# Moving the row numbers of the slots ahead of the attention's close, in the second of five rounds

## The reference

```python
h = _layernorm(x) * (1 + ca) + sa
o = mala_attn(q, k, v) + lepe_conv(v, lepe_w, lepe_b)   # num / den, plus a 5-tap convolution
x = x + ga * ((o * (h @ Wg.T)) @ Wo.T)
h = _layernorm(x) * (1 + cb) + sb
routing_weights = softmax(h @ router_weight.T)
_, top_idx = top_k(routing_weights + e_score_bias, 6)
top_w = routing_weights[top_idx] / sum(routing_weights[top_idx])
out = sum over the 6 experts of top_w * expert(h) + shared(h)
x = x + gb * out
```

## Time and profile before

| | |
|---|---|
| median of three timed executions | 889.64 us (878.7 to 890.82) |
| the profiled execution, time | 872.31 us |
| its span | 870.5 us |
| mean granted clock of TensorE | 0.953 |
| TensorE, VectorE, ScalarE, GpSimd busy | 88%, 55%, 46%, 47% of the span |

### The profile page before, as it was taken

One profiled execution on the slowest core, in us unless ns is written; L12 is line 12 of the kernel. 1 busy time (PEld: TensorE's weight loads), 2 busy tenths in 40 slices (PEclk: granted clock), 3 DMA queues, 4 the chain that ended last, 5 costly groups with the idle time before them and its releaser, 6 DMA issues.

```text
span 870.5 us, 13265 instructions
## 1 busy us (share of the span) xinstructions
PE 767.5 (88%) x4302; PEld 601.0 (69%) x4302; DVE 474.5 (55%) x1207; ACT 397.1 (46%) x943; POOL 410.5 (47%) x420
## 2 busy tenths in 40 slices
PE   5999999998888976799888898889999999999963
PEld 4666576575475644478787797888989988997421
DVE  3687788787489415334333343343444444445986
ACT  5585638644442622035445353544456555563000
POOL 0000002666657667456566566555556555666100
PEclk9999999999988978799899999999999999999996
DMA  9500010242248955435565765555565555568795
GB/s 329 165 1 0 1 49 37 99 162 114 113 176 302 356 206 215 140 136 188 176 209 174 247 202 195 178 184 172 172 207 186 168 187 189 184 204 337 279 413 226
DMA packets 82605, 158.45 MB, mean 182 GB/s; under 512 B 14430, under 2 KB 55523, under 8 KB 82280
## 3 DMA queue, kind: packets, MB, share of 16 engines
q1 hardware_dynamic: 58344, 96.74, 33.8%
q0 software_dynamic: 19968, 56.67, 16.5%
q10 hardware_dynamic: 4224, 4.19, 1.4%
HBM read 88.15 MB, written 73.57 MB: 186 GB/s over the span
## 4 chain that ended last, share of the span: by engine, by line
PE 65%; DVE 9%; ACT 8%; issue 7%; another core or an unknown queue 5%; DMA 3%; SPq 2%; ACTq 1%; DVEq 0%
PE ps_wide L1333 15%; PE ps_wide L1348 8%; PE ps_kv L1333 7%; PE ps_narrow L1321 5%; PE ps_wide L1093 5%; PE ps_wide L969 3%; PE ps_narrow L1106 2%; DMA arena<-expert_outs 2%; PE ps_wide L1115 2%; PE ps_wide L1101 2%; PE ps_kv L1115 2%; ACT arena L900 1%; PE ps_narrow L1045 1%; PE ps_wide L1086 1%
## 5 line engine op out<-in xcount | busy, mean ns | idle before, releaser
L544 POOL DMA_INDIRECT expert_rows<-arena,slot_i x192 | 192.5, 1003 | 239.4 <-DVE arena L1649 143.3
L650 POOL DMA_INDIRECT expert_outs<-arena,meta x224 | 217.8, 972 | 158.7 <-DVE arena L1854 106.9
L900 ACT COPY arena<-arena 128x512 f32 x224 | 127.3, 618 | 189.5 <-remote 95.9
L1854 DVE TENSOR_SCALAR arena<-ps_wide,meta 128x256 f32<-128x256 f32 x224 | 97.9, 479 | 172.8 <-PE ps_wide L1348 99.5
L1333 PE MATMUL ps_wide<-arena 128*128 128x128 f32 x1200 | 154.5, 281 | 13.5 <-ACT arena L883 6.6
L1333 PEld LDWEIGHTS ps_wide<-arena 128*128 128x128 f32 x1200 | 149.3, 196 | 24.2 <-ACT arena L883 11.6
L1348 PE MATMUL ps_wide<-arena 128*128 x448 | 117.9, 386 | 1.6 <-issue 1.6
L1348 PEld LDWEIGHTS ps_wide<-arena 128*128 128x128 f32 x448 | 77.8, 194 | 9.2 <-issue 3.1
L1333 PEld LDWEIGHTS ps_kv<-arena 128*128 128x128 f32 x592 | 72.4, 194 | 12.5 <-ACT arena L883 6.4
L1333 PE MATMUL ps_kv<-arena 128*128 128x128 f32 x592 | 74.7, 278 | 7.2 <-issue 3.5
L1093 PE MATMUL ps_wide<-arena 128*128 128x512 f32 x160 | 71.8, 594 | 2.8 <-DVE arena L1545 2.8
(11 more groups left out here) (235 smaller groups left out, 1046.6 us busy)
## 6 DMA issues: line engine op xcount, KB each, us to landing
arena<-expert_rows SPq DMA_DIRECT2D x224, 160.0 KB, 2.8
arena<-expert_outs SPq DMA_DIRECT2D x48, 512.0 KB, 15.8
arena<-w_experts SPq DMA_DIRECT2D x32, 384.0 KB
expert_rows<-pad_row SPq DMA_DIRECT2D x33, 160.0 KB
out<-x ACTq DMA_DIRECT2D x8, 512.0 KB, 10.2
expert_outs<-arena,meta POOLq DMA_INDIRECT x224
x<-x SPq DMA_DIRECT2D x3, 1024.0 KB, 11.0
h_cols<-arena SPq DMA_DIRECT2D x6, 512.0 KB
```

The lines of the kernel that those rows point to most:

```text
L544: nc.gpsimd.indirect_dma_start(rows, bass.IndirectOffsetOnAxis(ap=slots_i[b % 2][:, t, k:k + 1], axis=0), hrows[b % 2][:, t, :], None, bou ...
L650: nc.gpsimd.indirect_dma_start(outs, bass.IndirectOffsetOnAxis(ap=meta_i[:, j % METAS, 1:2], axis=0), yb[j % OUTS], None, bounds_check=las ...
L900: last = nc.scalar.copy(wgu[:, j % 4:j % 4 + 1, :], wall[:, bass.ds(expert[j], 1), 0:DOWN])
L1854: v.tensor_scalar(yb[j % OUTS], ps_wide[:, 1, p % 2, j % DUO * D:(j % DUO + 1) * D], meta[:, j % METAS, 0:1], None, ALU.mult).then_inc(s_y ...
```

## The change

On VectorE, `rows_of_slots()` of round b = 1 (the rows of batch 0) is called right behind `slots()`, ahead of `close_o(0)`. Rounds 2 and 3 keep it behind `close_o(1)`. Round 4 has no close and is as it was.

```diff
@@ -1749,6 +1749,8 @@
                     take_ranks()
                     spread_rden()
                     slots()
+                    if b == 1:
+                        rows_of_slots()
                 else:
                     shared_mid(0)
                     make_table(0, ps_narrow[:, 1])
@@ -1766,7 +1768,7 @@
                 if front:
                     close_o(0)
                     close_o(1)
-                    if hurry:
+                    if hurry and b > 1:
                         rows_of_slots()
                     add_o(0)
                     if tabled:
```

## The result

| | kernel before | changed kernel |
|---|---|---|
| median of 22 executions each | 881.9 us (865.76 to 891.31) | 883.96 us (875.7 to 890.79) |
| mean of the same | 881.6 us | 883.2 us |
| profiled execution: time, span | 872.31, 870.5 us | 878.44, 876.6 us |
| mean granted clock in it | 0.953 | 0.956 |

The ratio of the two kernels is 1.0088, with a 95% interval of 1.0049 to 1.0128; the verdict at 2% is "same". The medians differ by only 2.1 us (0.2%). The ratio counts, for each kernel, only the executions within 1.5% of its own fastest, and one execution of before at 865.76 us leaves 6 of its 22 against 20 of the changed kernel's 22; so I read its size, some 8 us, with care. The difference of the means of all executions is +1.6 us, with two standard errors of 3.4. The forecast was 892.8 us, a range of 879.5 to 896, and +3.2 us.

A forecast was written before the change was run, and what follows sets the result against it. TensorE was taken as the main bound, with VectorE's close_o(0) a link in the second round's chain; 1.46 + 0.03 + 1.7 = 3.2 us on a median of 889.64 gave 892.8 us, range 879.5 to 896.

The forecast's parts named there:

- close_o(0) is a link: Second round's attention close: delaying VectorE's first instruction of close_o(0) delays TensorE's project_out(0) and what follows.
- Delay of 1.46 us: VectorE, second round: the moved block starts close_o(0) 1.46 us later; the other 0.58 us fit into the broadcast wait.
- The clock falls, 1.7 us: TensorE before project_out(0), second round: a 2.74 us gap likely halves the granted clock, costing 1.7 us; chance 0.56.
- Zero for add_o, zero for the early signal: Behind the second round's closes: earlier add_o(0) and GpSimd starting 7.9 us earlier each gain nothing.
- Nothing downstream swallows it: Stages after the second round, expert weight loads and scatters included, shift by the whole 3.2 us.
- The clock holds: Rival, TensorE's gap before project_out(0): no clock loss, cost only 1.5 us, 891.1 us; chance 0.27.
- The scatters were the bound: Rival, GpSimd's scatter stream sets the stage's end and moves up 7.9 us: 881.7 us; chance 0.05.
- A stalled engine: Rival, last round's weight loads: a ScalarE wait for an unnamed release adds 19.5 us, 912.3 us in all; chance 0.05.
- Sum: Whole kernel: 1.46 delay, 0.03 for scatters beside close_o(0) and 1.7 clock make 3.2 us slower.

The follow-up runs named there:

- 20 us test: Kernel before plus nine unneeded VectorE reductions, some 20 us, ahead of close_o(0) of the second round; ratio 1.0254, means differ by 18.9 us.
- pair at 798 us: The kernel before and the changed kernel, both unchanged, measured and profiled again in a faster group; ratio 1.0035, means differ by +3.4 us.
- filler: Changed kernel plus five unneeded matmul calls in TensorE's gap before project_out(0), second round; L1133 to L1093 15.19 us, mean +2.7 us against the kernel before.
- Late scatters: Changed kernel with GpSimd also waiting for both closes of the second round before its first scatter; mean +3.2 us against the kernel before.

## Why the prediction was right, point by point

- **close_o(0) is a link.** Right. The 20 us test shows that most of a delay there reaches the end, and the pair at 798 us carries 3.12 us unchanged through two rounds.
- **Delay of 1.46 us.** Right in size where it was read: 1.45. In other executions it is 1.75, because VectorE waits only 0.33 us for the broadcasts instead of 0.61. The 0.61 stands where TensorE's clock had fallen just ahead of the broadcasts (0.79 from 126 to 134 us in the kernel before); where it had not (1.00 in the same kernel at 798 us) the wait is 0.33. I had taken one execution's cover as fixed.
- **The clock falls, 1.7 us.** Right: 5.38 - 3.70 = 1.68, and the filler takes exactly that away. It fell just as work resumed, as I had assumed for this price (its 3.4 us at 1.2 GHz are 3.3 by the two windows of rows 11, which leaves the 1.7), and it was 5.38 us in all four profiles with this gap in the second round (2.75, 3.03 twice, 3.04 us). With 1.28 us or less it fell in none. By those four I gave it too little chance. My reason, the length of the gap, was too simple: at 2.31 us in the fourth round it fell in ten of eleven unfilled profiles, at 2.45 us in the third round it held, and at 1.86 or 1.87 us in the first it held in four profiles and fell in one. The same gap behind the same work had both outcomes, so the length does not decide alone; what else does, no run here separates. The size of the price was in part luck: in the fourth round it ran from 1.5 to 3.0 us (5.20 to 6.68 us for the projection).
- **Zero for add_o, zero for the early signal.** Right. Late scatters changed nothing, and a first scatter 5.35 us later had been made up for by 201 us.
- **Nothing downstream swallows it.** Right within a few tenths up to the first load of expert rows at 798 us. In the totals it is less sure: of a delay of 23.2 us, 18.9 (3.5) arrived.
- **The rivals.** "The clock holds" is what the filler makes true, and it gave the 1.75 us. "The scatters were the bound" is wrong for the second round; for the fourth it holds 2.3 us. "A stalled engine": ScalarE's wait did not grow, 25.4 us in the changed kernel's profile against 28.54. Waits for unnamed releases as a whole hold 10% of its chain of waits against 5%, within the 5 to 13% of the other kernels near 880 us; that is no sign of the change, and no proof against one. The prediction called the DMA queues full beside that wait; between 342.4 and 359.9 us they took 38.0% and 6.6% of the engines' time.
- **Sum.** 3.2 forecast; 3.15 and 3.43 in place, 3.5 (2.3) in total at 798 us. The total alone would fit the rival's 1.5 as well; the place in the profiles decides between them.
- **The time itself.** 892.8 us was forecast and 883.96 measured, 8.8 less. That it lies in the range is owed to the range's width: the three executions that I started from had a median of 889.64, and 22 of them have 881.9.

The first comparison's 1.0088 would be 8 us. Up to the fourth round's broadcasts its profiles show 3.7, and the spans differ by 6.1, with unlike waits for unnamed releases between; with the same kernels 1.0035 was measured at 798 us. That part of it is the choice of executions is argued, not shown.

## What to carry to other kernels

Here a block behind the critical work on its engine cost nothing; ahead of it, it cost its length less the wait that it filled, and that wait has to be read in more than one execution. Before work is moved ahead for the sake of a consumer's earlier start, look at what the consumer waits for next: three scatters went 8 us earlier and then waited 12 us. And where TensorE waits for the moved work, price the clock along with the gap, and as a chance: the same gap lost it in one execution and not in another.

## What the runs showed of the hardware

**Two sources of different times that the change does not touch.** The first is TensorE's clock in the sparse stretches of a round. In the kernel with the block between the closes, a window of the third round's denominators (L1259, 128x4) reads

```profile
200.00:212.00 12.00, 12.00 (x47) 0.57 0.15 61
```

and VectorE's timeline of the same kernel shows who paid:

```profile
206.82 0.23 DVE L1674 TENSOR_SCALAR arena<-ps_wide 128x64 f32<-128x64 f32 x1 [5.27 <-PE ps_wide L1259]
```

TensorE was busy all of that time, and yet at the lower level for most of it. In the kernel before, the same stretch, from 190 to 200 us, had a clock of 1.00, and the stage took 67.5 us from L1133 to L1133 against 74.7 here, of which 1.7 are the block's place. In the first round the clock was at 0.50 from 60 to 66 us in nine of the fourteen profiles and at 1.00 in five; the second round's broadcasts start near 137 us in the nine and between 130 and 132 in the five.

The second is the wait for a release that the trace does not name. ScalarE's 28.54 us ended at 361.87. The queues of the kernel before, in the window from 359.9 to 361.0 us, hold one packet of an instruction queue:

```profile
q14 instruction: 1, 0.01, 3.5%
```

and between 342.4, when TensorE's matmuls for ScalarE were done, and 359.9 they hold none. A late load of code would look like this; only the timing speaks for it, and no run tests it. The Trainium skill (Runtime: NRT & Kernel Launch, "Instruction fetch mechanics") states that this fetch is mostly hidden; if these waits are that, it was not hidden in this execution. Over the whole of it the groups of waits (time in all, times, longest) have

```profile
ACT arena L900 <- remote: 95.9, 28, 6.3
DVE arena L1854 <- remote: 69.5, 21, 6.1
```

and at 798 us the same kernel has no wait for an unnamed release at all, though its instruction queues moved the same 35 and 34 packets; there L900 waits for TensorE:

```profile
ACT arena L900 <- PE ps_narrow L1321: 147.2, 109, 3.8
```

Such waits hold 5 to 13% of the chain of waits in all ten profiles of 870 to 899 us, and none of it in the four of 788 to 804 us. So they belong to the slower groups. They need not be the whole difference: in the kernel before they hold 5% of 870.5 us, some 44 us, and its two profiles are 72.8 us apart. What delays these releases was not tried, nor whether moving six instructions shifts VectorE's share of them.
